# Layer-norm rows of a one-layer language tower: split by token and turned by transposing DMAs in place of TensorE

## What is computed

```python
h = nan_to_num(take(embed_table, ids))            # 16384 rows of 256
x = layernorm(h)                                   # first layer norm
f, i = sigmoid(x @ Wf.T), sigmoid(x @ Wi.T)        # gates
g = where(x @ Wh.T >= 0, x @ Wh.T + 0.5, sigmoid(x @ Wh.T))
s[t] = f[t] * s[t-1] + i[t] * g[t]                 # scan along time, s[-1] = 0.5
h = h + s
x = layernorm(h)                                   # second layer norm
r = relu(bitlinear(x, w_fc) + gate * low_rank(x))  # 256 -> 1024, low rank 16
out = h + bitlinear(r * r, w_proj)                 # 1024 -> 256
```

## Time and profile before

| | us |
|---|---|
| median of 3 runs | 1036.16 |
| lowest, highest | 1035.92, 1037.06 |
| span of the profiled execution | 1033.3 |
| TensorE busy in it | 968.8 (94%) |
| VectorE busy | 864.6 (84%) |
| ScalarE busy | 553.0 (54%) |
| GpSimd busy | 489.6 (47%) |

### The profile page before, as it was taken

The page is one execution under the profiler, slowest core; times in us unless marked ns, Lnnn a source line. Parts: engine busy times, 40 slices in busy tenths (PEclk is TensorE's granted clock), DMA queues, the critical chain, the costliest instruction groups (busy, mean ns, idle before and its releaser), DMA issues.

```text
span 1033.3 us, 18090 instructions
## 1 busy us (share of the span) xinstructions
PE 968.8 (94%) x5825; PEld 582.6 (56%) x5825; DVE 864.6 (84%) x1570; ACT 553.0 (54%) x775; POOL 489.6 (47%) x427
## 2 busy tenths in 40 slices
PE   1779999999999999999999999999999999999987
PEld 1336655556655555665556566555656655566654
DVE  6897888888888888888888888888898888888673
ACT  3355566545556644555664455566445556545543
POOL 6525455445545544554554454555445455442210
PEclk9899999999999999999999999999999999999998
DMA  4000000000000000000000000000000000000001
GB/s 128 10 1 8 25 26 25 21 25 25 5 26 25 24 22 25 25 5 26 25 23 23 25 25 5 26 25 23 23 26 26 5 25 25 21 25 22 21 1 41
DMA packets 26582, 24.30 MB, mean 24 GB/s; under 512 B 5190, under 2 KB 25232, under 8 KB 26560
## 3 DMA queue, kind: packets, MB, share of 16 engines
q1 hardware_dynamic: 20416, 19.81, 5.8%
q0 software_dynamic: 6144, 4.21, 1.8%
HBM read 19.81 MB, written 16.78 MB: 35 GB/s over the span
## 4 chain that ended last, share of the span: by engine, by line
PE 44%; DVE 30%; issue 14%; POOL 6%; ACT 3%; DVEq 1%; DMA 1%; POOLq 1%; SPq 0%; ACTq 0%
PE y_ps L659 20%; PE bank L576 16%; DVE normed L741 6%; DVE hid L921 6%; DVE sq_hi L961 4%; POOL value L323 4%; DVE x_lo L747 3%; PE turned L645 3%; PE turned L493 3%; DVE cand L912 2%; DVE rows_pos L719 2%; ACT cand_lin L413 2%; DVE low L937 2%; DVE rows_neg L721 1%; POOL rstd L295 1%
## 5 line engine op out<-in xcount | busy, mean ns | idle before, releaser
L659 PE MATMUL y_ps<-proj_t,sq_hi 128*128 128x256 bf16 x1024 | 225.3, 273 | 0.0
L659 PE MATMUL y_ps<-proj_t,sq_lo 128*128 128x256 bf16 x1024 | 225.3, 273 | 0.0
L283 POOL DMA_INDIRECT rows_raw<-table,idx_now x128 | 184.8, 1444 | 58.3 <-issue 30.2
L623 PE MATMUL bank<-x_hi,fc_t 128*128 128x512 f16 x512 | 195.8, 382 | 0.7 <-issue 0.7
L625 PE MATMUL bank<-x_lo,fc_t 128*128 128x512 f16 x512 | 195.5, 382 | 0.0
L413 ACT ACTIVATE forget<-bank,w_back 128x512 f32<-128x512 f32 x64 | 44.0, 687 | 278.3 <-PE bank L576 278.3
L444 ACT ACTIVATE relu<-bank,relu_scale 128x512 f32<-128x512 f32 x256 | 164.5, 681 | 16.8 <-PE bank L629 16.8
L323 POOL TENSOR_TENSOR value<-inp,cand 128x512 f32<-128x512 f32 x64 | 81.9, 1279 | 187.2 <-DVE cand L912 187.2
L963 DVE TENSOR_TENSOR sq_lo<-sq,sq_hi 128x1024 f16<-128x1024 f32 x128 | 156.9, 1225 | 4.4
L741 DVE TENSOR_SCALAR normed<-h,moments,rstd 128x256 f32<-128x256 f32 x256 | 119.5, 529 | 43.5 <-POOL rstd L295 43.5
L576 PE MATMUL bank<-x_hi,w_hi 128*128 128x512 f16 x384 | 147.0, 383 | 2.4 <-issue 2.4
(11 more groups left out here) (140 smaller groups left out, 1348.1 us busy)
## 6 DMA issues: line engine op xcount, KB each, us to landing
out<-out_sb SPq DMA_DIRECT2D x32, 512.0 KB, 3.0
rows_raw<-table,idx_now POOLq DMA_INDIRECT x128, 3.0
fc_raw<-w_fc SPq DMA_DIRECT2D x1, 1024.0 KB, 7.0
pj_raw<-w_proj SPq DMA_DIRECT2D x1, 1024.0 KB, 9.1
w_raw<-wf SPq DMA_DIRECT2D x1, 256.0 KB, 3.2
w_raw<-wi SPq DMA_DIRECT2D x1, 256.0 KB, 3.5
w_raw<-wh SPq DMA_DIRECT2D x1, 256.0 KB, 4.1
ids_sb<-ids SPq DMA_DIRECT2D x1, 64.0 KB, 1.8
```

Of the source, the lines that this page charges most:

```text
L283: pool.indirect_dma_start(rows_raw[:, par, j, :], None, table, bass.IndirectOffsetOnAxis(ap=idx_now[:, par, j:j + 1], axis=0), bounds_chec ...
L623: pe.matmul(dst[:, :], fc_t[:, k, f * P:(f + 1) * P], x_hi[1][:, k, :], start=(k == 0), stop=False)
L659: ins = pe.matmul(y_ps[:, j, :], part[:, f, j * P:(j + 1) * P], proj_t[:, f, :], start=(f == 0 and j % 2 == 0 and part is sq_hi), stop=(f ...
```

## The change

The rows are split into halves by token, in SBUF, before they are turned: ScalarE writes the high half of `normed` (128 tokens x 4 tiles x 256), VectorE the low half. SyncE then issues one transposing DMA for each half, which writes the columns that TensorE reads (`x_cols`), double-buffered for the first norm. TensorE's `turn` disappears. hid's turn moves from behind fc tile 7 to behind fc tile 5 and no longer waits for x_hi and x_lo. low_rank moves from gate tile 3 to gate tile 4. On VectorE x_low of the first norm stands behind scan 0, x_low of the second norm directly behind its normalise and ahead of y_sb. On ScalarE x_high of the first norm stands behind the fifth activation, low_high behind the sixth, and x_high of the second norm at the end of the step. The guard bounds the rows in one instruction in place of two, and its second stage takes min with 0 and max with the bounded rows.

```diff
-        rows_pos = sb("rows_pos", [P, TILES, D])
-        rows_neg = sb("rows_neg", [P, TILES, D])
+        rows_fin = sb("rows_fin", [P, TILES, D])
...
-        x_hi = [sb(f"x_hi{k}", [P, KD, CHUNK], F16) for k in range(2)]
-        x_lo = [sb(f"x_lo{k}", [P, KD, CHUNK], F16) for k in range(2)]
+        x_rows = [sb(f"x_rows{k}", [P, 2, TILES, D], F16) for k in range(2)]
+        x_cols = [sb(f"x_cols{k}", [P, 2 - k, 2, TILES, KD, P], F16) for k in range(2)]
...
+        def x_part(k, par, part):
+            return x_cols[k][:, par, part, :, :, :]
...
@@ SyncE @@
+            def turn_rows(k, c, par):
+                for part, ready in enumerate((x_hi_ready[k], x_lo_ready[k])):
+                    sp.wait_ge(ready, c + 1)
+                    pass_on(sp, sp_passed, c)
+                    sp.dma_start_transpose(x_part(k, par, part).rearrange("p j k t -> p (j k) t"),
+                                           x_rows[k][:, part, :, :].rearrange("p j d -> p (j d)"))\
+                        .then_inc(x_landed[k], 16)
+            turn_rows(0, 0, 0)
             def step(n, h, par):
+                if known_below(n, N - 1):
+                    wait(sp, gate_done, 6 * n)
+                    pass_on(sp, sp_passed, n)
+                    turn_rows(0, n + 1, 1 - par)
+                if known_below(n, N):
+                    wait(sp, fc_done, FC * n)
+                    pass_on(sp, sp_passed, n)
+                    turn_rows(1, n, 0)
...
@@ GpSimd @@
             def clear(c, par):
-                wait(pool, raw_split, 2 * (c - 1))
+                wait(pool, h0_ready, c - 1)
...
@@ ScalarE @@
             def x_high(k, c):
-                act.wait_ge(x_turned[k], c + 1)
-                act.activation(x_hi[k][:, :, :], turned_cols, ACT.Copy).then_inc(x_hi_ready[k], 1)
+                act.wait_ge(normed_ready[k], TILES * (c + 1))
+                wait(act, x_landed[k], 32 * c)
+                act.activation(x_rows[k][:, 0, :, :], normed[k][:, :, :], ACT.Copy).then_inc(x_hi_ready[k], 1)
...
-                            if back and (e, q) == (0, 1):
-                                columns()
...
-                            if back and (e, q) == (1, 0):
+                            if (e, q) == (1, 0) and known_below(n, N - 1) and not (isinstance(n, int) and n == 1):
+                                x_high(0, n + 1)
+                            if back and (e, q) == (1, 1):
                                 low_high(m)
...
-                    if p == 1 and known_below(n, N - 1):
-                        act.wait_ge(gate_done, 6 * (n + 1))
-                        x_high(0, n + 1)
...
+                if front:
+                    x_high(1, n)
...
@@ TensorE @@
-            def turn(k, c):
...
-                        if back and p == 1:
-                            pe.wait_ge(h1_ready, n)
-                            turn(1, m)
-                        if back and p == 3:
+                        if back and p == 4:
                             low_rank(n, m, True)
...
-                    if f == 3 and known_below(n, N - 1) and not (isinstance(n, int) and n == 0):
-                        wait(pe, x_hi_ready[1], n)
-                        wait(pe, x_lo_ready[1], n)
-                        turn(0, n + 1)
...
-                if front:
-                    pe.wait_ge(scanned, 4 * (n + 1))
-                    ahead = min(n + 2, N) if isinstance(n, int) else n + 2
-                    pe.wait_ge(x_hi_ready[0], ahead)
-                    pe.wait_ge(x_lo_ready[0], ahead)
+                    if front and f == 5:
+                        pe.wait_ge(scanned, 4 * (n + 1))
+                        wait(pe, h1_ready, n)
...
@@ VectorE @@
-                dve.tensor_scalar(rows_pos[:, :, :], rows_raw[:, par, :, :], 0.0, FMAX, ALU.max, ALU.min)\
-                    .then_inc(raw_split, 1)
-                dve.tensor_scalar(rows_neg[:, :, :], rows_raw[:, par, :, :], 0.0, -FMAX, ALU.min, ALU.max)\
-                    .then_inc(raw_split, 1)
+                dve.tensor_scalar(rows_fin[:, :, :], rows_raw[:, par, :, :], -FMAX, FMAX, ALU.max, ALU.min)\
+                    .then_inc(raw_bounded, 1)
             def guard_sum(c, par):
-                dve.wait_ge(raw_split, 2 * (c + 1))
-                dve.tensor_tensor(h0[:, par, :, :], rows_pos[:, :, :], rows_neg[:, :, :], ALU.add).then_inc(h0_ready, 1)
+                dve.wait_ge(raw_bounded, c + 1)
+                dve.scalar_tensor_tensor(h0[:, par, :, :], rows_raw[:, par, :, :], 0.0, rows_fin[:, :, :],
+                                         ALU.min, ALU.max).then_inc(h0_ready, 1)
...
             def x_low(k, c):
                 dve.wait_ge(x_hi_ready[k], c + 1)
-                dve.tensor_tensor(x_lo[k][:, :, :], turned_cols, x_hi[k][:, :, :], ALU.subtract)\
+                dve.tensor_tensor(x_rows[k][:, 1, :, :], normed[k][:, :, :], x_rows[k][:, 0, :, :], ALU.subtract)\
                     .then_inc(x_lo_ready[k], 1)
...
                 if front:
                     scan(0)
+                if known_below(n, N - 1) and not (isinstance(n, int) and n <= 1):
+                    x_low(0, n + 1)
...
                 if front:
                     normalise(1, n, h1[:, par, :, :])
+                if front:
+                    x_low(1, n)
```

More of the change, by code:

```diff
@@ L486, in low_rank_product @@
                         .then_inc(anorm_spread, 1)
-            def turn(k, c):
-                pe.wait_ge(normed_ready[k], TILES * (c + 1))
-                for e in range(KD):
-                    for j in range(TILES):
-                        ins = pe.transpose(turned_cols[:, e, j * P:(j + 1) * P],
-                                           normed[k][:, j, e * P:(e + 1) * P], ident[:, :])
-                ins.then_inc(x_turned[k], 1)
-            turn(0, 0)
             def turn_bound():
@@ L549, in low_rank @@
                 for k in range(KD):
-                    pe.matmul(bank[0][:, :], low_a[:, k, :], x_hi[1][:, k, :], start=(k == 0), stop=False)
-                    ins = pe.matmul(bank[0][:, :], low_a[:, k, :], x_lo[1][:, k, :], start=False, stop=(k == KD - 1))
+                    for part in range(2):
+                        ins = pe.matmul(bank[0][:, :], low_a[:, k, :], x_part(1, 0, part)[:, :, k, :],
+                                        start=(k == 0 and part == 0), stop=(k == KD - 1 and part == 1))
                 ins.then_inc(low_done, 1)
@@ L574, in step @@
                             for w in (w_hi, w_lo):
-                                for x in (x_hi, x_lo):
-                                    ins = pe.matmul(bank[gate_bank[p]][:, :], w[:, k, q, :], x[0][:, k, :],
-                                                    start=(k == 0 and w is w_hi and x is x_hi),
-                                                    stop=(k == KD - 1 and w is w_lo and x is x_lo))
+                                for part in range(2):
+                                    ins = pe.matmul(bank[gate_bank[p]][:, :], w[:, k, q, :],
+                                                    x_part(0, par, part)[:, :, k, :],
+                                                    start=(k == 0 and w is w_hi and part == 0),
+                                                    stop=(k == KD - 1 and w is w_lo and part == 1))
                         ins.then_inc(gate_done, 1)
-                        if back and p == 1:
-                            pe.wait_ge(h1_ready, n)
-                            turn(1, m)
-                        if back and p == 3:
+                        if back and p == 4:
                             low_rank(n, m, True)
@@ L622, in step @@
                         for k in range(KD):
-                            pe.matmul(dst[:, :], fc_t[:, k, f * P:(f + 1) * P], x_hi[1][:, k, :],
-                                      start=(k == 0), stop=False)
-                            pe.matmul(dst[:, :], fc_t[:, k, f * P:(f + 1) * P], x_lo[1][:, k, :],
-                                      start=False, stop=False)
+                            for part in range(2):
+                                pe.matmul(dst[:, :], fc_t[:, k, f * P:(f + 1) * P], x_part(1, 0, part)[:, :, k, :],
+                                          start=(k == 0 and part == 0), stop=False)
                         if f == 0:
@@ L964, in step @@
                                           sq_hi[:, 2 * p:2 * p + 2, :], ALU.subtract).then_inc(sq_lo_ready, 1)
-                    if p == 1 and known_below(n, N - 1) and not (isinstance(n, int) and n == 0):
-                        dve.wait_ge(gate_done, 6 * (n + 1))
+                    if p == 1 and first:
                         x_low(0, n + 1)
```

42 lines of the change are left out of this document (16 added, 26 removed).

## The result

The changed kernel takes 1168.35 us (median of 4 runs, 1168.03 to 1168.85), against 1036.32 (1035.92 to 1037.06) for the kernel before beside it: a ratio of 1.1278, 95% interval 1.1262 to 1.1294. It is slower by 132 us, where the forecast was 69. The range of 1055 to 1210 holds it, the forecast's own range (1085 to 1130) does not.

A forecast was written before the change was run, and what follows sets the result against it. TensorE and VectorE were taken to hand the bound to each other in every step. 29 rounds of 2.2 us more (64) plus 4 for the ends, 68 on a span of 1033.3, led to 1105 us; own range 1085 to 1130, wider 1055 to 1210.

The forecast's parts named there:

- The wait of x_low(1) for the copy: On VectorE behind layer norm 1's normalise: a first new wait of 1.1 us for ScalarE's high half.
- The wait of normalise(0) for rstd: On VectorE: a second new wait, 1.35 us, for GpSimd's rstd of the next chunk behind its output addition.
- Guard: On VectorE: one of two instructions goes, worth 0.61 us; the second stage takes 1.2 us.
- The rest of TensorE: TensorE rests some 4 us for low before fc tile 0's last matmul.
- The landing: Transposing DMAs land in 4.1 us, hidden behind TensorE's wait for low, costing 0 us.
- a mark of being wrong: Listed signs against the forecast: TensorE resting for a DMA, granted clock under 0.95 mid-run, or h1's additions under 30 apart.
- The DMA rival: Layer norm 1's transposing DMAs land too late: 1398 us one behind the other, 1169 if overlapping; chance 18%.
- The ends: First chunk's and last chunk's columns lie bare: 4 us together (0 to 10).
- The clock in the f phase: TensorE's fc tiles after low were laid out at 0.216 us a matmul, from 19.9 to 28.35.
- the rival that had the right price: TensorE's rest before the f phase lowers its clock, up to about 2 us a step: 1105 to 1165; chance 17%.
- The 3.68 from out_sb's start to rstd's end: On GpSimd: output addition from 10.6, rstd ready 3.68 us later at 14.3, setting normalise(0)'s start.
- The third wait: On VectorE near the round's end: a new wait of 1.05 us for ScalarE's last square.

The follow-up runs named there:

- e1_y_first: The changed kernel with VectorE's y_sb moved ahead of layer norm 1's x_low: 1099.18 us, ratio 1.0624.
- e6_y_first_fill: The changed kernel with y_sb ahead of layer norm 1's x_low, plus 8 useless matmuls in TensorE's rest before low: 1077.22 us, ratio 1.0405.
- e4_dma_twice: The changed kernel with each transposing DMA of layer norm 1 preceded by a twin into unused memory, TensorE waiting for all four: 1148.29 us, ratio 1.1117.
- e2_fill: The changed kernel with 16 useless matmuls put before fc tile 0's wait for low: 1120.52 us, ratio 1.0834.
- e9_norm_first: e7_reordered with normalise(0) ahead of the first cand, second cand ahead of low, low_rank and low_high behind the last gate tile, among other moves: 1143.75 us.
- e7_reordered: The changed kernel with y_sb first, hid's turn last, chunk n+2's measuring and rstd earlier, guard behind the second cand: 1041.44 us, ratio 1.0043.
- e12_out_later: e7_reordered with layer norm 1's copy behind the next step's first activation and GpSimd's output addition behind its first value: 1058.54 us, ratio 1.0225.
- e11_measure_ahead: The changed kernel with only chunk n+2's measuring moved behind guard_sum and its rstd ahead of the output addition: 1116.35 us, ratio 1.0775.

## Why the prediction was right in sign and half in size

Right, point by point:

- The wait of x_low(1) for the copy: 1.20 (1.1). The wait of normalise(0) for rstd: 1.24 (1.35). Guard: its second stage 1.19 (1.2), one instruction less. That y_sb standing behind the waiting x_low is what carries the lateness to GpSimd and back is shown by e1_y_first and e6_y_first_fill: 1.4 us a round.
- The rest of TensorE: 3.96 ("some 4 us"). The landing: 3.2 (4.1), hidden; e4_dma_twice made it 3 us later without moving `low`. TensorE did rest 0.98 for the columns, which the list in the prediction has as a mark of being wrong, but that rest only takes from the longer one before `low`, and the sum had it so (columns wanted at 11.8, there at 13.4). The DMA rival's figure for overlapping transfers, 1169, is met by accident: its landing of 18.4 never came near. Another of its marks, a granted clock under 0.95 in the middle (0.86 and 0.77), did come, and it points at what follows. By "VectorE: DVE Perf Modes" of the Trainium skill, section on the three transpose paths, eight blocks were an estimated 10.5 us; the runs show 3.2, so its time for one block doesn't scale to eight.
- The ends: 5.1 us (4).

Wrong, and by how much:

- **The clock in the f phase** is the step that failed. The sum laid fc tiles 0 to 7 out at 0.216 us a matmul, from 19.9 to 28.35, directly behind a rest that it had itself forecast at 4 us; the rival that had the right price stood beside it at 17%. Measured: matmuls about 0.4 us apart for two tiles, 1.59 us in a mean round (e2_fill against the changed kernel), 48 us in all. As the earlier trace rows had shown the same thing after 3.78 us of rest, that rival should have been the forecast: 1105 + 30 x 1.7 = 1156.
- **normalise(0)** starts at 14.81, not 14.3. The 3.68 from out_sb's start to rstd's end was carried over from the earlier trace rows, but in its new place var_eps runs beside cand: 0.67 instead of 0.23. That is 0.5 of the 2.70 that e2_fill leaves, 15 us; it is read from the traces, and no run tests it by itself.
- The third wait was taken as one of 1.05 behind the last square. At full clock it is 0.90 (e2_fill); in the changed kernel it is spread over four pairs, since all fc tiles are late.

Together: 69 forecast, 48 of clock and 15 of later rstd, make 132 (the differences in the ends and in the third wait nearly cancel). The range from 1055 to 1210 holds the total because it was drawn to take in the rivals, not because of the sum. Open is why a rest of 2.5 us brings the clock down in every second round and not in each, and why one of 3.77 in e4_dma_twice didn't; why a fall lasts longer in e9_norm_first; and how far the slow normalise depends on which of the two engines started first. Not tried: an output addition that overlaps neither cand nor normalise, the one way that this reading leaves for e7_reordered to become faster than both kernels. The best version is the kernel before with the new guard, 1030.15 us.

## What to carry to other kernels

A rest that your own sum gives to TensorE has to be carried on into the speed of what comes behind it: look in the trace for a rest of that length and price what came behind it as a rival at least; here rests of 2.3 to 4.0 us were followed by a fall in some rounds or in all, those of 1.3 and 1.8 in e7_reordered and e12_out_later by none (granted clock 1.00 from 400 to 1000 us in both). When work moves from a fast engine to a DMA, the new price is often the queue position of the elementwise instructions that now must finish before it, not the transfer: one that waits holds all behind it (here y_sb, for 1.4 us a round). And an instruction's duration belongs to its neighbours on the other engine: before moving one, read what will run beside it there.

## What the runs showed that was not expected

GpSimd and VectorE hold each other off. Normalise of four tiles (f32, in SBUF) takes 1.35 to 1.38 with GpSimd at rest, 2.32 beside value, 4.35 and 4.42 beside value and out_sb. (The four stay back to back; single ones of them take up to 2.44.) In e12_out_later the two engines' work laid end to end is 1.38 + 1.26 + 2.39 = 5.0, and they took 4.42 together. GpSimd loses too: out_sb took 2.35 to 3.34, according to what VectorE did. "SBUF — State Buffer" of the Trainium skill, section "SBUF: two separate sides", describes a port pair that VectorE and GpSimd share as an exclusive lock; by that rule, the durations agree nearly, though not in full. This explains most of the miss of e12_out_later and about half of those of e7_reordered (the other half is cand's wait of 1.09) and e11_measure_ahead (the other half is the clock).

TensorE's useless work can shorten a kernel: 16 matmuls in each round took 47.8 us off, 8 of them 22.0 (1099.18 to 1077.22).

SyncE needs 1.3 us to issue one transposing DMA (1.23 to 1.33 singly in e4_dma_twice, against 0.4 for a store). In the changed kernel's timeline, the two of layer norm 1:

```profile
521.41 2.61 SPq L255 DMA_TRANSPOSE x_cols<-x_rows  x2
```
